# Routed experts of a decoder layer: norm folded into the resident expert weights, turned rows moved by VectorE, a third expert buffer, replies in 4 KB runs

## The chip, the cores and the metric

The kernel runs on one core of a Trainium2 chip. The metric is the device time of one execution in microseconds (us), lower is better. All tensors are float32.

## The reference, cut to what matters

A two-layer decoder on x of 32 batches x 112 tokens x 256 features (3584 tokens). Each layer has a causal attention, an attention over a context of 375 rows, and a feed-forward with experts. The change touches only the last step, the second half of layer 1's feed-forward: 32 experts of 256 -> 128 -> 256, of which each token uses the 4 with the highest score.

```python
x2 = _layernorm(src, ln2_g, ln2_b)           # (s - mean) * rsqrt(var + 1e-5) * g + b
sel = jax.nn.sigmoid(x2 @ sel_w)             # 256 x 32
scores, idx = jax.lax.top_k(sel, K)          # K = 4
gate = (jax.nn.one_hot(idx, E) * scores[..., None]).sum(-2)
h = jax.nn.relu(jnp.einsum('bsd,edh->bseh', x2, keys))      # keys 32 x 256 x 128
moe_out = jnp.einsum('bseh,ehd,bse->bsd', h, values, gate)  # values 32 x 128 x 256
return src + moe_out
```

The output is x + that return value.

## The kernel before, in words

`routed_experts` (line 2488) runs last, in one block with a program per engine. X holds the decoder's residual, S the inner stream (`src`), both resident as 112 partitions x 32 batches x 256. Engines meet only at semaphores, and each engine and each DMA queue takes its program in order. The stage has three parts.

**Choosing and sending.** Eight chunks c of 4 batches. VectorE measures (`measure`, 2740) and normalises without gain and bias (`scale`, 2749), which also adds S to X; the power -0.5 is on GpSimd (`power`, 2586). TensorE turns the rows (2620), ScalarE evicts them with the gain and bias of the norm (2683), TensorE routes (2627), ScalarE takes the sigmoid (2687), VectorE finds the four experts and each token's slot in that expert's region (`choose`, 2760), with two ranking matmuls of TensorE between (2631). ScalarE copies every row four times (2692), VectorE tags the copies with reply place and score (2793, 2794), and GpSimd sends them with indirect DMAs into the table of slots in HBM (`send`, 2590): 16 a chunk, 128 in all, each of 112 rows x 1032 bytes. Meanwhile SP's queue loads the resident `weights` of all 32 experts: 128 partitions x 32 experts x 512 (two halves of keys, 128 each, and 256 of values). The stage starts with SP's small loads; VectorE waits for them (2733) ahead of everything it does.

**The expert tiles.** 143 tiles (`TILES`) of 128 rows. Which expert a tile has is known only at run time, from `table`. For tile j:
- SP: reads the address from the table (2564) and loads 128 x 1032 bytes into one of R = 8 places of `rows` (2569).
- VectorE: reads the expert's number into a register (2822), copies this expert's 128 x 512 weights to one of two buffers `expert` (2824), and takes the minimum that makes the reply addresses (2826). The copy waits for `answered`: the buffer of tile j is free when down(j - 2) is done.
- TensorE: `turn(j)`, two transposes (2648); `up(j)`, two matmuls (2656); `down(j)`, one matmul (2663). A float32 matmul shows as two records. The order is written out: turn(j + 2), up(j + 1), down(j).
- ScalarE: `tile(j)`, two evictions of the turned rows with the norm's gain and bias (2700) into one of two `tileT`; `hide(j)`, the ReLU (2707); `reply(j)`, the scaled eviction of the answer (2712). The order is tile(j + 2), hide(j + 1), reply(j).
- GpSimd: sends the 128 replies with an indirect DMA to their places in HBM (2608).

```python
for j in range(TILES):                 # TensorE, 2669
    if j + 2 < TILES: turn(j + 2)
    if j + 1 < TILES: up(j + 1)
    down(j)
```

**The combine.** When all replies have landed, SP loads the 4 replies of each token of a batch (2575; 112 x 4 runs of 1 KB, 448 KB), six batches ahead; VectorE adds them in three instructions (2832, 2834, 2835), and ScalarE's queue writes the batch out (2727, 112 KB).

Of the kernel before, what the change touches and what calls it, by code (L numbers as in the profile page):

```python
# [26 lines left out]
ACT = mybir.ActivationFunctionType  # L27
# [2460 lines left out]
def routed_experts(nc, G, layer1, W1):  # L2488
# [6 lines left out]
    with ExitStack() as stack:  # L2495
        sb, psum, sem = G["alloc"](stack, "m1")
        weights, route, ln = sb("weights", [P, E, 512]), sb("route", [P, DC, E]), sb("ln", [P, 2, DC])
        rows = sb("rows", [P, 8 * ROOM, D + 2])
        xn, xT = sb("xn", [P, Q, D]), sb("xT", [P, DC, Q * T])
# [13 lines left out]
        expert = [W1["aq"], W1["akc"]]  # L2513
        tileT = [W1["cq"], W1["ck"]]
# [18 lines left out]
        chain_sem, once = sem("chain"), sem("once")  # L2533
        block = stack.enter_context(nc.Block())
# [20 lines left out]
        def _(sp):  # L2555
# [56 lines left out]
        def _(pe):  # L2612
            pe.wait_ge(small_loaded, 16 * len(smalls))
            pe.wait_ge(restart_set, 4)
            for c in range(NC):
# [9 lines left out]
                for i in range(Q):  # L2625
                    for f in range(DC):
# [7 lines left out]
                                 start=False, stop=True).then_inc(ranked, 1)  # L2634

# [15 lines left out]
            def up(j):  # L2651
# [3 lines left out]
                for f in range(DC):  # L2655
                    ins = nc.tensor.matmul(bank[6 + j % 2][:, 0:P], expert[j % 2][:, f * P:(f + 1) * P], tileT[j % 2][:, f, 0:P],  # L2656
# [3 lines left out]
            def down(j):  # L2660
                pe.wait_ge(hidden_ready, j + 1)
                at_least(pe, reply_ready, j - 1)
                nc.tensor.matmul(bank[j % 2][:, 0:D], hidden[j % 2], expert[j % 2][:, DC * P:512],  # L2663
# [13 lines left out]
        def _(act):  # L2677
# [37 lines left out]
            tile(0)  # L2715
            tile(1)
            hide(0)
            for j in range(TILES):
                if j + 2 < TILES:
                    tile(j + 2)  # L2720
# [10 lines left out]
        def _(dve):  # L2731
            chain = Chain(dve, chain_sem, once=once)
            dve.wait_ge(small_loaded, 16 * len(smalls))
            dve.wait_ge(restart_set, 4)
# [25 lines left out]
            def choose(c):  # L2760
                dve.wait_ge(score_ready, c + 1)
# [37 lines left out]
            for c in range(NC):  # L2799
# [3 lines left out]
                if c + 1 < NC:  # L2803
                    scale(c + 1)
# [65 lines left out]
```

## Time and profile before

| | us |
|---|---|
| median of 3 timed runs | 3645.9 (3644.9 to 3647.05) |
| time of the profiled execution | 3625.27 |
| its span, first to last instruction | 3623.5 |
| sending, first to last send (2595) starting | 3106.8 to 3279.5 of the span |
| expert tiles, first to last reply (2712) starting | 3290.3 to 3550.5 |
| combine, first to last addition (2832) starting | 3559.1 to 3617.95 |

Times in a trace are microseconds from the span's start. PE is TensorE's matmul row, PEld its weight loads, DVE VectorE, ACT ScalarE, POOL GpSimd, SP SyncE; a name with q (DVEq, SPq) is the sequencer of that engine, which issues instructions and DMAs. A row of a timeline gives start, duration, engine, line, operation and tiles; what stands in brackets is how long the engine was idle before and what released it.

### The profile page before, as it was taken

What the parts mean: (1) busy time and instruction counts of PE and PEld (TensorE: products, weight loads), DVE (VectorE), ACT (ScalarE), POOL (GpSimd) and SP (SyncE); (2) the same over time, 40 slices, a digit from 0 to 9 for tenths busy, and PEclk for the clock granted to TensorE, in tenths of its full rate; (3) what the DMA queues carried; (4) which work ended last, traced back from release to release, by engine and by line L of the source; (5) the groups of instructions that cost most, each with busy time, mean ns of one, the idle gap of its engine ahead of it and who ended that gap; (6) DMA issues with size and microseconds to landing.
All of it is one profiled execution on the core that took longest, in us unless ns stands there. A gap on an engine that the chain in (4) does not pass through costs nothing. (4 is left out here: it accounts for less than half of the span.)

```text
span 3623.5 us, 79765 instructions
## 1 busy us (share of the span) xinstructions
PE 3014.6 (83%) x28616; PEld 2127.2 (59%) x28616; DVE 2215.9 (61%) x4462; ACT 1774.6 (49%) x3526; POOL 514.2 (14%) x728
## 2 busy tenths in 40 slices
PE   6997999999999978999995799888878998225771
PEld 5885555555555546667774566656647887224551
DVE  4996566666666645667774566656636887552225
ACT  3775555555555532324442344434436887225771
POOL 0000111111111100000000000000001110575551
PEclk9998999999999988999998999999988999558996
DMA  7000544444444410000001333323206776524448
GB/s 174 0 0 22 168 137 137 137 137 137 137 137 137 137 42 1 0 0 1 0 0 38 63 66 67 64 63 67 61 17 202 233 232 187 155 84 128 144 145 226
DMA packets 327192, 351.23 MB, mean 97 GB/s; under 512 B 104552, under 2 KB 304368, under 8 KB 326864
## 3 DMA queue, kind: packets, MB, share of 16 engines
q1 hardware_dynamic: 188304, 174.78, 18.5%
q10 hardware_dynamic: 125680, 140.22, 13.0%
q0 software_dynamic: 13008, 33.56, 2.8%
q8 instruction: 126, 2.06, 0.2%
q14 instruction: 74, 0.61, 0.1%
HBM read 109.49 MB, written 207.08 MB: 87 GB/s over the span
## 5 line engine op out<-in xcount | busy, mean ns | idle before, releaser
L1817 DVE TENSOR_REDUCE x_top<-x_scores 112x4 f32<-112x1500 f32 x128 | 219.9, 1718 | 242.5 <-PE x_scores L1673 239.2
L1054 ACT ACTIVATE x_probs<-x_held,x_minus_top 112x488 f32<-112x488 f32 x256 | 177.5, 694 | 264.4 <-DVE x_minus_top L1111 264.4
L732 POOL TENSOR_TENSOR x_rstd<-x_var,g_minus_half 112x1 f32<-112x1 f32 x128 | 77.9, 609 | 1475.9 <-DVE x_var L728 1008.1
L960 PE MATMUL x_ring<-w_xkv,x_kv 128*122 128x512 f32 x512 | 233.4, 599 | 15.7 <-ACT x_k L844 15.0
L953 PE MATMUL x_ring<-x_kv,w_xkv 128*128 128x488 f32 x512 | 241.6, 596 | 0.0
L1778 ACT ACTIVATE x_probsT<-x_scores 125x1792 f32<-125x1792 f32 x96 | 159.7, 1664 | 147.2 <-PE x_scores L1692 144.6
L844 ACT ACTIVATE x_v<-x_ring 122x512 f32<-122x512 f32 (+1 forms) x224 | 109.8, 506 | 231.7 <-PE x_ring L960 181.4
L1105 DVE SCALAR_TENSOR_TENSOR x_held<-x_scores,x_keep 112x976 f32<-112x976 f32 x128 | 150.4, 1175 | 112.6 <-PE x_scores L973 105.6
L960 PEld LDWEIGHTS x_ring<-w_xkv,x_kv 128*122 128x122 f32 x512 | 92.2, 185 | 137.2 <-issue 94.1
L953 PEld LDWEIGHTS x_ring<-x_kv,w_xkv 128*128 128x128 f32 x512 | 88.0, 191 | 126.2 <-issue 126.0
L2608 POOL DMA_INDIRECT expert_replies<-m_rows,m_reply_of x143 | 137.3, 960 | 135.6 <-DVE m_reply_of L2826 128.4
L1110 DVE TENSOR_REDUCE x_top<-x_held 112x2 f32<-112x976 f32 x128 | 149.7, 1170 | 4.4
L981 PEld LDWEIGHTS x_ring<-g_constants,x_probs 112*122 112x122 f32 x1024 | 109.6, 139 | 71.0 <-issue 65.3
L1673 PE MATMUL x_scores<-x_slots 32*112 32x375 f32 x1024 | 118.3, 531 | 37.1 <-ACT x_probsT L1778 22.4
L2482 DVE SCALAR_TENSOR_TENSOR g_residual<-m_out,m_gate,g_residual 112x256 f32 (+1 forms) x256 | 107.7, 477 | 66.1 <-PE m_out L2326 64.4
L1692 PE MATMUL x_scores<-x_q,x_slots 32*125 32x112 f32 x3072 | 114.1, 286 | 35.4 <-DVE x_top L1817 32.8
L973 PE MATMUL x_scores<-x_k,x_q 64*112 64x488 f32 x512 | 137.8, 615 | 0.8 <-PEq L229 0.8
L2595 POOL DMA_INDIRECT expert_slots<-m_rows,m_slot_of x128 | 129.1, 1009 | 49.2 <-issue 35.9
L1692 PEld LDWEIGHTS x_scores<-x_q,x_slots 32*125 32x125 f32 x3072 | 99.0, 190 | 57.4 <-issue 50.4
L1138 DVE TENSOR_TENSOR x_normed<-x_ring,x_inverse_rows 128x224 f32<-128x224 f32 x64 | 25.1, 391 | 173.4 <-PE x_ring L998 173.4
L981 PE MATMUL x_ring<-g_constants,x_probs 112*122 112x112 f32 x1024 | 120.8, 261 | 5.8 <-ACT x_probsT L844 3.8
L844 ACT ACTIVATE x_probsT<-x_ring 122x448 f32<-122x448 f32 x256 | 123.5, 535 | 0.9 <-PE x_ring L981 0.9
(351 smaller groups left out, 7320.1 us busy)
## 6 DMA issues: line engine op xcount, KB each, us to landing
expert_slots<-d_empty ACTq DMA_DIRECT2D x32, 3612.0 KB, 14.1
by_position<-r_by_position SPq DMA_DIRECT2D x64, 784.0 KB, 4.3
r_bias<-by_position SPq DMA_DIRECT2D x64, 392.0 KB, 3.4
x_ctx<-in_ctx SPq DMA_DIRECT2D x64, 375.0 KB
m_rows<-expert_slots SPq DMA_DIRECT2D x143, 129.0 KB, 2.1
x_kq_swapped<-x_kq_raw ACTq DMA_DIRECT2D x64, 243.5 KB, 3.6
x_slots<-x_kq SPq DMA_DIRECT2D x512, 30.4 KB
m_rows<-expert_replies SPq DMA_DIRECT2D x32, 448.0 KB, 9.7
```

The source lines that it names most:

```text
L844: self.ring.freed(self.nc.scalar.activation(dst, src_of(bank), ACT.Copy), c)
L953: ins = nc.tensor.matmul(bank[:, 0:XK], W["xkv"][:, f, m * P:(m + 1) * P], self.kv[:, f, :], start=(f == 0), stop=(f == DC - 1))
L960: ins = nc.tensor.matmul(bank[0:XCK, :], self.kv[:, f, i * XCK:(i + 1) * XCK], W["xkv"][:, f, 512:1024], start=(f == 0), stop=(f == DC - 1))
L973: ins = nc.tensor.matmul(self.scores[0:T, at:at + XK], self.q[par][half, m, :], self.k[par][half, m, :], start=True, stop=True)
L981: ins = nc.tensor.transpose(bank[0:XCK, i * T:(i + 1) * T], self.probs[u % 4][0:T, i * XCK:(i + 1) * XCK], self.const("ident", T)[:, 0:T])
L1054: nc.scalar.activation(self.probs[u % 4][0:T, :], self.held[m % 2][0:T, i, :], ACT.Exp, scale=self.scale, bias=self.minus_top[0:T, m % 2, ...
L1105: nc.vector.scalar_tensor_tensor(self.held[m % 2][0:T, :, :], self.scores[0:T, 1024 * (m % 2):1024 * (m % 2 + 1)].rearrange("t (i c) -> t ...
L1110: chain.link(nc.vector.tensor_reduce(self.top[0:T, m % 2, :], self.held[m % 2][0:T, :, :], AX_X, ALU.max))
L1692: ins = nc.tensor.matmul(self.scores[0:CK, 512 * a + g * T:512 * a + (g + 1) * T], slots[slot, g, i * CK:(i + 1) * CK], self.q[slot, g, :] ...
L1778: self.nc.scalar.activation(self.probsT[0:CK, i, :, :], self.scores[0:CK, :].rearrange("t (a c) -> t a c", c=512)[:, :, 0:HG * T], ACT.Exp ...
L1817: nc.vector.tensor_reduce(self.top[0:T, g, :], self.scores[0:T, :].rearrange("t (a c) -> t a c", c=512)[:, :, 0:S2], AX_X, ALU.max).then_i ...
L2608: pool.indirect_dma_start(replies[:, :], bass.IndirectOffsetOnAxis(reply_of[:, j:j + 1], 0), rows[:, R + j % R, 0:D], None).then_inc(repli ...
```

## The change

- The norm's gain and bias leave the tiles: `tile` on ScalarE goes, the gain is multiplied into the resident keys (two VectorE instructions in each of chunks 2 to 5), and the bias's part of each hidden unit is made once per expert by 64 matmuls of one column (16 in each of chunks 2 to 5, after the ranking matmuls). Each tile copies its expert's bias column (VectorE), and `hide` adds it in the ReLU. The routing's eviction (2683) keeps gain and bias.
- VectorE moves the turned rows from PSUM to `tileT`, as the last step of a function `bring(j)` that holds all that it does for a tile.
- `expert` has three buffers: the copy for tile j waits for down(j - 3).
- VectorE's wait for the small loads stands in `choose(0)`, after measure and scale of chunk 0.
- The combine's loads land in contiguous 4 KB per token, in place of four runs of 1 KB placed 1032 bytes apart.

```diff
+        groups = rows[:].rearrange("p (g k) d -> p g (k d)", k=K)[0:T, :, 0:K * D]
...
-        expert = [W1["aq"], W1["akc"]]
-        tileT = [W1["cq"], W1["ck"]]
+        expert = [W1["aq"], W1["akc"], sb("expert2", [P, 512])]
+        tileT = [W1[n][:].rearrange("p c n -> p (c n)")[:, 0:D] for n in ("cq", "ck")]
+        bias_of, bias = sb("bias_of", [P, E]), sb("bias", [P, 4])
...
         # SP, combine
-                sp.dma_start(rows[0:T, 4 * g:4 * g + 4, 0:D],
-                             replies[b * T * K:(b + 1) * T * K, :].rearrange("(t k) d -> t k d", k=K)).then_inc(gathered[g], 16)
+                sp.dma_start(groups[:, g, :],
+                             replies[b * T * K:(b + 1) * T * K, :].rearrange("(t k) d -> t (k d)", k=K)).then_inc(gathered[g], 16)
...
         # TensorE, chunk c, after the ranking matmuls
+                if 2 <= c < 6:
+                    if c == 2:
+                        pe.wait_ge(weights_loaded, 16 * len(larges))
+                    for e in range(EG * (c - 2), EG * (c - 1)):
+                        for f in range(DC):
+                            ins = nc.tensor.matmul(bank[7][:, e:e + 1], weights[:, e, f * P:(f + 1) * P], ln[:, 1, f:f + 1],
+                                                   start=(f == 0), stop=(f == DC - 1))
+                    ins.then_inc(folded, 1)
...
         # ScalarE
-            def tile(j):
-                act.wait_ge(tile_turned, j + 1)
-                at_least(act, hidden_full, j - 1)
-                for f in range(DC):
-                    ins = nc.scalar.activation(tileT[j % 2][:, f, 0:P], bank[4 + j % 2][:, f * P:(f + 1) * P], ACT.Identity,
-                                               bias=ln[:, 1, f:f + 1], scale=ln[:, 0, f:f + 1])
-                ins.then_inc(tile_ready, 1)
...
-                nc.scalar.activation(hidden[j % 2], bank[6 + j % 2][:, 0:P], ACT.Relu).then_inc(hidden_ready, 1)
+                nc.scalar.activation(hidden[j % 2], bank[6 + j % 2][:, 0:P], ACT.Relu,
+                                     bias=bias[:, j % 4:j % 4 + 1]).then_inc(hidden_ready, 1)
...
         # VectorE: start, chunk c, tiles
-            dve.wait_ge(small_loaded, 16 * len(smalls))
-            dve.wait_ge(restart_set, 4)
...
+                if 2 <= c < 6:
+                    dve.wait_ge(folded, c - 1)
+                    these = slice(EG * (c - 2), EG * (c - 1))
+                    for f in range(DC):
+                        ins = nc.vector.tensor_scalar(weights[:, these, f * P:(f + 1) * P], weights[:, these, f * P:(f + 1) * P],
+                                                      ln[:, 0, f:f + 1], None, ALU.mult)
+                    ins.then_inc(scaled, 1)
+                    nc.vector.tensor_copy(bias_of[:, these], bank[7][:, these]).then_inc(biased, 1)
...
+            def bring(j):
+                which = dve.value_load(table[0:1, 0, j:j + 1], min_val=0, max_val=E - 1)
+                at_least(dve, answered, j - 2)
+                nc.vector.tensor_copy(expert[j % 3][:], weights[:, bass.ds(which, 1), :].rearrange("p e n -> p (e n)"))
+                nc.vector.tensor_copy(bias[:, j % 4:j % 4 + 1], bias_of[:, bass.ds(which, 1)]).then_inc(expert_ready, 1)
+                dve.wait_ge(loaded[j % R], 16 * (j // R + 1))
+                nc.vector.tensor_tensor(reply_of[:, j:j + 1], rows[:, j % R, D:D + 1], part("limit")[:, j:j + 1],
+                                        ALU.min).then_inc(reply_listed, 1)
+                dve.wait_ge(tile_turned, j + 1)
+                at_least(dve, hidden_full, j - 1)
+                nc.vector.tensor_copy(tileT[j % 2], bank[4 + j % 2][:, 0:D]).then_inc(tile_ready, 1)
```

## Rows read from the trace of the kernel before

**Rows 1.** Windows: PE, PEld, DVE, ACT, POOL busy; clock; DMA share; GB/s.
```profile
3082.00:3281.00 199.00, 50.74 (x232) 43.47 (x232) 92.09 (x346) 45.81 (x57) 137.92 (x140) 0.50 0.39 118
3300.00:3550.00 250.00, 181.45 (x1086) 139.40 (x1086) 72.60 (x272) 196.30 (x543) 130.49 (x137) 1.00 0.47 142
3560.00:3620.00 60.00, 0.00 (x0) 0.00 (x0) 48.54 (x95) 0.00 (x0) 0.00 (x0) 0.50 1.06 288
```
**Rows 2.** Timeline, one tile in the middle of the expert tiles.
```profile
3395.72 0.44 DVE L2824 COPY w_akc<-m_weights 128x512 f32 x1 [1.30 <-PE m_bank L2663]
...
3396.77 0.60 PE L2663 MATMUL m_bank<-w_aq,w_cv 128*128 128x256 f32 x2
3396.84 0.96 POOL L2608 DMA_INDIRECT expert_replies<-m_rows,m_reply_of  x1 [0.91 <-DVE m_reply_of L2826]
...
3397.21 0.38 PE L2648 MATMUL m_bank<-g_constants,m_rows 128*128 128x128 f32 x2
...
3397.52 0.51 DVE L2824 COPY w_aq<-m_weights 128x512 f32 x1 [1.30 <-PE m_bank L2663]
...
3398.13 0.68 PE L2656 MATMUL m_bank<-w_cq,w_aq 128*128 128x128 f32 x4 [0.54 <-issue]
...
3398.65 0.60 PE L2663 MATMUL m_bank<-w_akc,w_cv 128*128 128x256 f32 x2
```
**Rows 3.** All instructions of line 2712 (duration min/median/max, first and last start).
```profile
L2712 ACT ACTIVATE m_rows<-m_bank,m_rows x143: 473/474/477, 3290.3 to 3550.5; 128x256 f32<-128x256 f32 x143
```
**Rows 4.** Timeline, the last two replies: GpSimd with work waiting.
```profile
3551.11 0.96 POOL L2608 DMA_INDIRECT expert_replies<-m_rows,m_reply_of  x1 [0.83 <-ACT m_rows L2712]
3552.37 0.96 POOL L2608 DMA_INDIRECT expert_replies<-m_rows,m_reply_of  x1 [0.30 <-issue]
```
**Rows 5.** Lines 2826 and 2822 (VectorE's minimum, its sequencer) and 2569 (SP's).
```profile
L2826 DVE TENSOR_TENSOR m_reply_of<-m_rows,w_wp x143: 139/141/160, 3285.3 to 3548.5; 128x1 int32<-128x1 f32 x143
L2822 DVEq TENSOR_LOAD <-m_table x143: 299/304/551, 3259.3 to 3546.4; - x143
L2822 DVEq FUSED_REGOPS  x143: 190/190/207, 3259.9 to 3546.7; - x143
L2569 SPq DMA_DIRECT2D m_rows<-expert_slots x143: 332/333/363, 3283.2 to 3537.7; - x143
```
**Rows 6.** Lines 1138 and 1150: VectorE instructions that read PSUM.
```profile
L1138 DVE TENSOR_TENSOR x_normed<-x_ring,x_inverse_rows x64: 383/392/393, 401.6 to 1340.9; 128x224 f32<-128x224 f32 x64
L1150 DVE TENSOR_SCALAR w_ob<-x_ring,x_mv,x_rstd x32: 543/544/547, 425.3 to 1348.2; 112x256 f32<-112x256 f32 x32
```
**Rows 7.** Timeline, sending: GpSimd beside VectorE, chunk 1.
```profile
3129.64 1.22 DVE L2757 TENSOR_TENSOR g_residual<-g_residual,l_stream 112x1024 f32<-112x1024 f32 x1
3129.78 1.76 PE L2620 MATMUL m_bank<-g_constants,m_xn 112*128 112x112 f32 x8 [11.04 <-DVE m_xn L2754]
3129.91 1.77 POOL L2595 DMA_INDIRECT expert_slots<-m_rows,m_slot_of  x1 [0.30 <-issue]
```
**Rows 8.** Line 2036: VectorE, a column of factors, one input in SBUF.
```profile
L2036 DVE TENSOR_SCALAR r_xn<-l_stream,r_rstd x32: 343/344/354, 2720.2 to 3039.3; 112x256 f32 x24, 112x256 f32<-112x256 f32 x8
```
**Rows 9.** Timeline, TensorE's weight loads at the half clock.
```profile
3290.94 0.93 PEld L2656 LDWEIGHTS m_bank<-w_cq,w_aq 128*128 128x128 f32 x4 [0.62 <-issue]
```
**Rows 10.** Timeline, the start of the stage.
```profile
3082.27 0.20 POOL L2580 MEMSET w_ao<- 128x128 f32 x1 [46.68 <-POOLq L260]
...
3086.71 1.40 DVE L2742 BATCH_NORM_STATS2 m_stats<-l_stream 112x6 f32<-112x256 f32 x4 [5.35 <-DMA m_ln<-in_L_ffn_ln_b]
...
3106.82 1.16 POOL L2595 DMA_INDIRECT expert_slots<-m_rows,m_slot_of  x1 [11.14 <-DVE m_rows L2794]
```
**Rows 11.** Timeline, the combine: first addition, one without a wait, last.
```profile
3559.12 0.69 DVE L2832 TENSOR_TENSOR m_rows<-m_rows 112x512 f32<-112x512 f32 x1 [10.43 <-DMA m_rows<-expert_replies]
...
3617.95 0.69 DVE L2832 TENSOR_TENSOR m_rows<-m_rows 112x512 f32<-112x512 f32 x1
```
**Rows 12.** Who waited for whom, from 3556 us to the end.
```profile
DVE m_rows L2832 <- DMA m_rows<-expert_replies: 18.8, 27, 10.4
```

More of the change, by code:

```diff
@@ L2533, in routed_experts @@
         chain_sem, once = sem("chain"), sem("once")
+        folded, biased, scaled = sem("folded"), sem("biased"), sem("scaled")
+        EG = E // 4
         block = stack.enter_context(nc.Block())
@@ L2655, in up @@
                 for f in range(DC):
-                    ins = nc.tensor.matmul(bank[6 + j % 2][:, 0:P], expert[j % 2][:, f * P:(f + 1) * P], tileT[j % 2][:, f, 0:P],
+                    ins = nc.tensor.matmul(bank[6 + j % 2][:, 0:P], expert[j % 3][:, f * P:(f + 1) * P], tileT[j % 2][:, f * P:(f + 1) * P],
                                            start=(f == 0), stop=(f == DC - 1))
@@ L2662, in down @@
                 at_least(pe, reply_ready, j - 1)
-                nc.tensor.matmul(bank[j % 2][:, 0:D], hidden[j % 2], expert[j % 2][:, DC * P:512],
+                nc.tensor.matmul(bank[j % 2][:, 0:D], hidden[j % 2], expert[j % 3][:, DC * P:512],
                                  start=True, stop=True).then_inc(answered, 1)
@@ L2713, in reply @@
                                      scale=rows[:, j % R, D + 1:D + 2]).then_inc(reply_ready, 1)
-            tile(0)
-            tile(1)
             hide(0)
             for j in range(TILES):
-                if j + 2 < TILES:
-                    tile(j + 2)
                 if j + 1 < TILES:
@@ L2760, in choose @@
             def choose(c):
+                if c == 0:
+                    dve.wait_ge(small_loaded, 16 * len(smalls))
+                    dve.wait_ge(restart_set, 4)
                 dve.wait_ge(score_ready, c + 1)
@@ L2820, in _ @@
             dve.wait_ge(weights_loaded, 16 * len(larges))
-            for j in range(TILES):
-                which = dve.value_load(table[0:1, 0, j:j + 1], min_val=0, max_val=E - 1)
-                at_least(dve, answered, j - 1)
-                nc.vector.tensor_copy(expert[j % 2][:], weights[:, bass.ds(which, 1), :].rearrange("p e n -> p (e n)")).then_inc(expert_ready, 1)
-                dve.wait_ge(loaded[j % R], 16 * (j // R + 1))
-                nc.vector.tensor_tensor(reply_of[:, j:j + 1], rows[:, j % R, D:D + 1], part("limit")[:, j:j + 1], ALU.min).then_inc(reply_listed, 1)
+            dve.wait_ge(scaled, 4)
+            dve.wait_ge(biased, 4)
+            def bring(j):
[9 more added lines that the diff above has]
+                nc.vector.tensor_copy(tileT[j % 2], bank[4 + j % 2][:, 0:D]).then_inc(tile_ready, 1)
+            for j in range(TILES):
+                bring(j)
             dve.wait_ge(summed, NC)
@@ L2831, in _ @@
                 dve.wait_ge(gathered[g], 16 * (b // 6 + 1))
-                chain.link(nc.vector.tensor_tensor(rows[0:T, 4 * g:4 * g + 2, 0:D], rows[0:T, 4 * g:4 * g + 2, 0:D],
-                                                   rows[0:T, 4 * g + 2:4 * g + 4, 0:D], ALU.add))
-                chain.link(nc.vector.tensor_tensor(X[0:T, b, :], X[0:T, b, :], rows[0:T, 4 * g, 0:D], ALU.add))
-                nc.vector.tensor_tensor(X[0:T, b, :], X[0:T, b, :], rows[0:T, 4 * g + 1, 0:D], ALU.add).then_inc(added, 1)
+                chain.link(nc.vector.tensor_tensor(groups[:, g, 0:2 * D], groups[:, g, 0:2 * D], groups[:, g, 2 * D:4 * D], ALU.add))
+                chain.link(nc.vector.tensor_tensor(X[0:T, b, :], X[0:T, b, :], groups[:, g, 0:D], ALU.add))
+                nc.vector.tensor_tensor(X[0:T, b, :], X[0:T, b, :], groups[:, g, D:2 * D], ALU.add).then_inc(added, 1)
 _TRANSPOSED = {"v_wT": "L0_attn_v_w", "o_wT": "L0_attn_o_w", "x_qT": "L1_xattn_Wq", "x_kT": "L1_xattn_Wk",
```

## The prediction

> **What bounds the kernel now.** I cut the stage into its three parts first [rows 1]. The window of the expert tiles shows no engine full: in 250 us ScalarE is busy 196.3, PE 181.5, GpSimd 130.5, VectorE 72.6. With nothing full, a ring of waits must set the pace, so I read the timeline of one tile [rows 2]. down(j) starts at 3396.77 and lasts 0.60; VectorE's expert copy, idle for 1.30, is released by it at 3397.52; it ends at 3398.03; up(j+2) starts 0.10 later; the next down, behind this up, starts at 3398.65. So each tile pays down 0.60 + hop 0.15 + copy 0.51 + hop 0.10 + up, start to the down behind it, 0.52 = 1.88 us, with the shorter copies of the other tiles (0.44) some 1.80. The rows of the scaled eviction give the mean: (3550.5 - 3290.3) / 142 = 1.832 us a tile [rows 3]. Two buffers make that ring: copy(j+2) needs down(j), and down(j+1) stands on PE behind up(j+2).
>
> In the sending part GpSimd is busy 137.9 of 199 us [rows 1], and the gap behind each send is 0.30 [rows 7]: with 128 gaps and the start of the stage taken off, it has no time to spare. The combine is paced by VectorE and its loads: 31 steps take 3617.95 - 3559.12 = 58.8 us, 1.898 each [rows 11], of which 18.8 - 10.4 = 8.4 us are waits for loads after the first [rows 12].
>
> **The tiles after the change.** The old ring opens: copy(j+3) needs down(j), and behind up(j+3) on PE stands down(j+2). It now gives two tiles: down 0.60 + 0.15 + what `bring` does + 0.06 to 0.10 + 0.52. In `bring` between the wait and the tile's release are the expert copy 0.44 to 0.51 [rows 2], the bias copy and the minimum, 0.14 each [rows 5], and the copy of 256 columns out of PSUM. That last one no row has. From below, an addition that reads 224 columns there takes 0.392; from above, a two-factor scaling of 256 takes 0.544 [rows 6]; I take 0.42, near the simpler instruction. Sum 1.14 to 1.33, so the ring is 2.43 to 2.70 us for two tiles: 1.22 to 1.35 a tile, less what the copies overlap.
>
> Four other limits stand close to it.
> - GpSimd: the last two replies show it with work waiting: 3552.37 - 3551.11 = 1.26 us a reply [rows 4]. 143 replies cannot go faster; this is the floor.
> - PE: up 0.52 and down 0.44, start to start [rows 2]; for the two transposes, whose successor always waited, 0.25 (two starts 0.11 apart within a 0.38 row) to 0.38. 1.21 to 1.34 at the full clock that it has in this window [rows 1].
> - VectorE: 1.14 to 1.33 of work, and its sequencer's register load 0.30 + 0.19 [rows 5] can run beside the last copy.
> - SP: 0.33 to issue a load [rows 5] and a register load that I take like VectorE's, 0.30 + 0.19, together 0.82 and small steps: about 1.0.
>
> ScalarE loses two evictions, 2 x 0.45, and keeps under 0.8; a bias operand in the ReLU I cost at nothing, as these 2 x 0.45 rows carried one. DMA works at share 0.47 now [rows 1]; at 1.3 us a tile that is 0.47 x 1.832 / 1.3 = 0.66, and loads are eight tiles ahead, so I cost it at nothing; if that cover went, PE's transposes would be late next. I take GpSimd's 1.26 and 0.05 for meetings with VectorE: **1.31 us a tile**, bounds 1.26 and 1.50. Gain 142 x (1.832 - 1.31) = **74.1 us** (81.2 to 47.1). Also the first tile's two evictions, 0.81, become minimum and copy: 0.4 us gained.
>
> Where the bound 1.50 comes from: in these rows the expert copy that started 0.68 us into a reply's send took 0.51, and others took 0.44 [rows 2], so the two meet somewhere, and a send that began inside VectorE's 1.22 us addition took 1.77 where replies take 0.96 and ended only 0.82 us after that addition [rows 7]. Serial sums are 0.96 + 0.51 = 1.47 a tile. But the copy started while the send ran and lost only 0.07, so the send holds what they share for about the first 0.75 us; 0.75 + 0.44 = 1.19 still fits under 1.26. The Trainium skill (SBUF — State Buffer, the sections on the shared port) speaks against this change: a Vector copy in a two-port mode and a GpSimd instruction exclude each other for the whole instruction, and descriptor writing stops. By it the sum would have the serial 1.47; in the trace the copy starts before the send has ended, so I keep it as a rival.
>
> **The folding.** PE gets 16 matmuls a chunk, of two records each: 32 weight loads of 0.93 / 4 = 0.23 us at the half clock [rows 9], 7.5 us. PE idles 11.0 us ahead of the next chunk's transposes [rows 7], which follow exactly there, so I cost them at nothing; beyond 11.0 the transposes would be late. VectorE gets two scalings of 1024 columns and a small copy. A one-factor scaling of 256 takes 0.344 [rows 8]. If it were one column a cycle like the 1.22 us addition of 1024, a scaling is 1.2; if it runs at twice that, as the row hints (an addition of 224 takes 0.392), 0.75. Both lie ahead of the next `choose`, in an idle stretch of some 3 us. What costs is that GpSimd cannot begin a send inside them: the addition above cost it some 1.77 - 0.96 = 0.81. Four chunks with one such meeting of 0.75: **3.0 us lost**, between 0 and two meetings each of 0.7, 5.6.
>
> **The start.** VectorE begins at 3086.71, held 5.35 us by the small loads, while the block starts about 3082.3 [rows 10]. The measuring, the power and the scaling now run in these 4.4 us; PE and ScalarE still wait for the loads, at the same 3086.7, and by then the rows are ready but for 0.5. First send at 3102.4 in place of 3106.82, and GpSimd paces the rest: **4.4 us gained**, 4.0 to 4.6. The queues are moved past nothing.
>
> **The combine.** VectorE's three instructions are unchanged in size: 0.69 + 0.43 + 0.42 and gaps, 58.8 less 8.4 = 50.4 for 31, 1.63 each. If loads were never late the gain is 8.4; if run length did nothing, 0. The loads queue six deep at 288 GB/s [rows 1], so bytes are what they wait for, and longer runs drop three of four packets. I take 1.70 a step: **6.1 us gained**. The Trainium skill (DMA: Bandwidth & Descriptors, Specifications) puts line rate at runs of 512 B and more; by it 1 KB is long enough and the gain would be 0. No row here has these loads in other runs.
>
> **Sum**: 74.1 + 0.4 + 4.4 + 6.1 - 3.0 = 82.0. The profiled execution took 3625.3 and would take 3543.3; the timed median stands 20.6 above it (0.57%), and nothing says that this belongs to what goes, so 3645.9 - 82.0 = **3563.9 us**.
>
> **Rivals.**
> - A, the forecast: GpSimd's queue sets the tiles, 1.31. Chance 0.59.
> - B, as A, but the combine gains nothing, bytes and not packets being its limit: 3645.9 - 75.9 = 3570.0. For it: 448 + 112 KB in 1.9 us is already 300 GB/s. Against: it is not VectorE's floor. 0.18.
> - C, VectorE and GpSimd exclude each other, 1.50 a tile and 5.6 lost in the folding: 47.1 + 0.4 + 4.4 + 6.1 - 5.6 = 52.4, 3593.5. For it: the 1.77. Against: the copy within a send. 0.17.
> - D, the change does not do what it says: the ring is closed again by the second `tileT` buffer at 1.83, as both copies now stand in one queue. Gain 7.9: 3638.0. Against: up(j+1), which frees it, is two tiles back. 0.02.
> - E, slower: VectorE becomes the bound with nothing overlapping. A register load of 0.52, copies 0.51 + 0.14 + 0.14 + 0.54 and two hops of 0.15 are 2.15 us; with 0.12 of address steps 2.27. That is 142 x 0.44 = 62 us more, less 7.9: 3700. It decides from 1.832 + 7.9 / 142 = 1.89 us a tile. Against: the register load has ended long before VectorE is released, after 1.30 us idle [rows 2]. 0.04.
>
> A measurement of this kernel tells 0.2%, 7.3 us, from no change. Faster by more: A to D, 0.95 with the edge of D taken off; within: 0.01; slower: E, 0.04. The range 3548 to 3592 takes in A's bounds (1.26 a tile, combine 8.4, nothing lost: 3551.4, and 3 us for the unknown gap between profile and median), B, and all of C but its end.
>
> **What would show it.** Right: replies (2712) 1.26 to 1.36 apart, GpSimd's gaps near 0.30 there with the releaser no longer VectorE's minimum, VectorE's wait ahead of the expert copy gone or short, the PSUM copy near 0.42; first send near 3102; combine steps near 1.70. Wrong: sends (2608) longer than 0.96 or expert copies longer than 0.51 on average (C); replies over 1.4 apart with VectorE busy or its sequencer loading (E); TensorE's transposes in chunks 3 to 6 late after the folding.

## The result, and the profile after

Timed side by side, the changed kernel took 3627.3 us (median of 5, 3625.0 to 3631.7) and the kernel before 3644.9 (median of 5, 3640.7 to 3647.1). The ratio is 0.9962, with a 95% interval of 0.9946 to 0.9978: 17.6 us gained by the medians, 14 by the ratio, where I forecast 82.0, and outside my range. The profiled execution took 3627.28 us, span 3625.5. That of before took 3625.27, 20 us less than its timed runs, so between the two profiles nothing is gained: the after one is 2.0 us longer.

The windows of the three parts (sending, tiles, combine), columns as in [rows 1]:
```profile
3078.00:3302.00 224.00, 77.57 (x360) 70.69 (x360) 97.68 (x359) 45.29 (x57) 135.68 (x139) 0.50 0.35 104
3313.00:3557.00 244.00, 189.96 (x1130) 150.45 (x1128) 129.16 (x560) 113.17 (x285) 136.44 (x141) 0.95 0.50 151
3566.00:3620.00 54.00, 0.00 (x0) 0.00 (x0) 46.98 (x94) 0.00 (x0) 0.00 (x0) 0.50 1.02 317
```
Sending got longer, the tiles only a little shorter, and still no engine is full in the tiles: VectorE went from 72.6 us busy in 250 to 129.2 in 244, ScalarE from 196.3 to 113.2. GpSimd, which I wanted full, is busy 136 of 244 us.

Lines of the kernel after (duration min/median/max in ns, first and last start): scaled eviction, replies, PSUM copy, scaling of the keys, ReLU with bias.
```profile
L2717 ACT ACTIVATE m_rows<-m_bank,m_rows x143: 465/474/477, 3313.5 to 3556.9; 128x256 f32<-128x256 f32 x143
L2612 POOL DMA_INDIRECT expert_replies<-m_rows,m_reply_of x143: 954/960/1162, 3314.8 to 3559.2; - x143
L2844 DVE COPY w_cq<-m_bank x72: 410/417/426, 3308.6 to 3554.6; 128x256 f32<-128x256 f32 x72
L2811 DVE TENSOR_SCALAR m_weights<-m_weights,m_ln x8: 746/750/754, 3165.3 to 3247.6; 128x1024 f32<-128x1024 f32 x8
L2711 ACT ACTIVATE w_cv<-m_bank,m_bias x143: 358/367/370, 3311.4 to 3555.8; 128x128 f32<-128x128 f32 x143
```
The prices of single instructions are as costed: the copy out of PSUM 0.417 (I took 0.42), the scaling 0.75, a reply 0.960 in the median. The ReLU, which I cost at no more than before, takes 0.367 for 0.277. The pace is not as costed: (3556.9 - 3313.5) / 142 = 1.714 us a tile, where I forecast 1.31 and [rows 3] gave 1.832.

Start and combine, answering to [rows 10, 11]:
```profile
3077.84 0.20 POOL L2584 MEMSET w_ao<- 128x128 f32 x1 [47.46 <-POOLq L260]
...
3098.11 1.16 POOL L2599 DMA_INDIRECT expert_slots<-m_rows,m_slot_of  x1 [11.24 <-DVE m_rows L2796]
...
3565.46 0.69 DVE L2853 TENSOR_TENSOR m_rows<-m_rows 112x512 f32<-112x512 f32 x1 [10.48 <-DMA m_rows<-expert_replies]
...
3619.98 0.68 DVE L2853 TENSOR_TENSOR m_rows<-m_rows 112x512 f32<-112x512 f32 x1
```
From the first memset to the first send it is 20.27 us in place of 24.55, 4.3 gained. The combine takes 54.5 / 31 = 1.758 a step in place of 1.898, 4.3 gained.

The loss is in the sending: 128 sends in 203.9 us (3098.1 to 3302.0) where before needed 172.6. The timeline from 3137 us, with the folding's last matmuls, the transposes, GpSimd's last send of this chunk, and what starts after it ("remote" in brackets: a semaphore event ended the wait, but no instruction ended near it):
```profile
3137.80 0.99 PE L2644 MATMUL m_bank<-m_ln,m_weights 128*128 128x1 f32 x4
...
3143.20 1.75 PE L2624 MATMUL m_bank<-g_constants,m_xn 112*128 112x112 f32 x8 [4.41 <-DVE m_xn L2753]
...
3161.60 0.94 POOL L2599 DMA_INDIRECT expert_slots<-m_rows,m_slot_of  x1 [0.30 <-issue]
3165.28 1.42 DVE L2811 TENSOR_SCALAR m_weights<-m_weights,m_ln 128x1024 f32<-128x1024 f32 x2 [21.00 <-remote]
3166.08 1.34 ACT L2695 ACTIVATE m_xT<-m_bank,m_ln 128x448 f32<-128x448 f32 x2 [31.88 <-remote]
...
3180.09 1.07 POOL L2599 DMA_INDIRECT expert_slots<-m_rows,m_slot_of  x1 [10.16 <-DVE m_rows L2796]
```
TensorE's last matmul of this chunk's folding ended at 3138.79. VectorE, which waits for that alone and has been idle for 21.0 us, starts 26.5 us later. ScalarE starts late too, after transposes that ended near 3144.9. In between GpSimd has sent without a break, 0.30 us from one send to the next; both are released 2.7 and 3.5 us after its last send ended, and GpSimd, out of work, has by then begun 17.5 us of idling. The same comes again at 3245 us (17.4 us). In the tiles it shows in small: 40 of the 143 ReLUs start over 0.3 us after the matmul that releases them has ended, in the profile before none. I call these **late releases**: TensorE's matmul has ended, and the engine waiting for it is released late. The trace also records the increments of the semaphores, and they put the delay into the increment, not into the waiting engine: that of the folding's semaphore stands at 3165.26, 26.5 us after the last matmul of the folding and 0.02 ahead of VectorE's start. The granted clock is 0.50 in the sending both before and after; in the tiles it is 0.95 for 1.00.

The 2.0 us between the spans add up: layers before 4.4 shorter, start 4.3, tiles 142 x (1.832 - 1.714) = 16.8, the step from them to the combine 0.1 and the combine 4.3 gained; sending 31.3 and the step from it to the tiles 0.6 lost.

### The profile page after: what moved, and what is told of

The parts are those of the page before. It is cut to its first block and busy times, and to the rows that moved or that the text cites. A ratio compares the mean times of both kernels' runs of the same rounds, so it can differ in the third digit from the quotient of the medians.

```text
span 3625.5 us, 80177 instructions
## 1 busy us (share of the span) xinstructions
PE 3037.6 (84%) x28744; PEld 2155.7 (59%) x28744; DVE 2276.2 (63%) x4760; ACT 1681.0 (46%) x3240; POOL 514.7 (14%) x728
## 5 line engine op out<-in xcount | busy, mean ns | idle before, releaser
L1054 ACT ACTIVATE x_probs<-x_held,x_minus_top 112x488 f32<-112x488 f32 x256 | 177.5, 694 | 264.3 <-DVE x_minus_top L1111 264.3
```

Of the source, the lines that this page charges most:

```text
L1054: nc.scalar.activation(self.probs[u % 4][0:T, :], self.held[m % 2][0:T, i, :], ACT.Exp, scale=self.scale, bias=self.minus_top[0:T, m % 2, ...
```

## The experiments

They went to several chips, each set with its own timed runs of the kernel before beside it. Two conditions came up, on the same kernels: in some sets no late releases, in others (also the first timing) many. One of the chips showed both, in different sets, so it is not the chip alone. I say "prompt" and "late" for them below. The table gives medians in us; in set x and for z's fourth kernel it is one timed run, elsewhere 2 to 11. The sets were run in the order of the table.

| set | condition | before | kernels |
|---|---|---|---|
| first timing | late | 3644.9 | changed 3627.3 |
| x | prompt | 3633.8 | x1 3549.4, x2 3625.9, x3 3551.0, x4 3527.7 |
| y | prompt | 3621.3 | changed 3536.1, y6 3533.8 |
| z | prompt | 3622.7 | changed 3542.7, z2 3534.6, z3 3546.6, before 3624.4 |
| w | prompt | 3621.1 | changed 3542.6, w2 3539.9 |
| v | late | 3636.3 | changed 3631.8, v2 3608.3 |
| u | late | 3646.4 | before 3639.9, u2 3555.4 |
| t | late | 3646.4 | t1 3621.7, t2 3607.6 |

**Set x: what in the change is slow?** x1 takes the 64 folding matmuls out of the changed kernel and sets the hidden bias to zero (the norm's bias is left out); the scalings stay.
```diff
...
-                    for e in range(EG * (c - 2), EG * (c - 1)):
-                        for f in range(DC):
-                            ins = nc.tensor.matmul(bank[7][:, e:e + 1], ...)
-                    ins.then_inc(folded, 1)
...
-                    nc.vector.tensor_copy(bias_of[:, these], bank[7][:, these]).then_inc(biased, 1)
+                    nc.vector.memset(bias_of[:, these], 0.0).then_inc(biased, 1)
```


> The changed kernel without the 64 one-column matmuls of the folding; the scalings stay, the bias of the hidden units is left out (set to zero). Theory H (TensorE's semaphore increments are held back while GpSimd issues sends one behind the other, once TensorE has done a long run of matmuls beside them): the two stalls of 20 us and the one of 6 us in the sending part go, first to last send takes 170 to 176 us in place of 203.9, and the tiles keep their pace of about 1.70 us, since nothing changes there. Rival W (VectorE's scalings of the weights keep the port from GpSimd or delay VectorE itself): the sending part stays above 190 us.

Measured: 84 us faster than before, sending 177.4, but tiles at 1.261: the slow tiles were gone with matmuls that had ended long before them, which no theory of mine had. x2 puts the same 64 matmuls alone into the kernel before.

> The kernel before with the 64 one-column matmuls of the folding added on TensorE and nothing else (their result is not used). Theory H: the sending part, 172.7 us before, grows by 20 to 35 us, with stalls in which TensorE has finished and VectorE and ScalarE still wait; the tiles stay at 1.83 us. Rival W: no change, within 2 us of 172.7, because the matmuls fit into the 11 us that TensorE idles.

Measured: sending 172.4 us, tiles 1.830, no late release, so theory H fell here. The matmuls cost what I had costed, in TensorE's idle time:
```profile
3138.37 6.82 PE L2641 MATMUL m_bank<-m_ln,m_weights 128*128 128x1 f32 x32
```
x3 is the kernel before with the third buffer alone.
```diff
-        expert = [W1["aq"], W1["akc"]]
+        expert = [W1["aq"], W1["akc"], sb("expert2", [P, 512])]
...
-                at_least(dve, answered, j - 1)
+                at_least(dve, answered, j - 2)
```


> The kernel before with three expert buffers and nothing else. If the ring of two buffers is what paced the tiles, the next limit is ScalarE with 0.80 + 0.28 + 0.47 us of evictions and its gaps: 1.58 to 1.65 us a tile in place of 1.83, some 30 us gained, with few late releases, as GpSimd then still has gaps of over 0.6 us between its replies. If late releases of TensorE's increments depend on TensorE's own density, they show here too and the pace stays above 1.70.

Measured: 82.8 us gained, 1.242 a tile; far more than I expected by then. x4 is the changed kernel with each tile's replies written in one piece by a plain DMA of ScalarE's queue, GpSimd idle in the tiles. It leaves out the placing of the replies: the same bytes are moved, but the combine adds wrong rows. (The edit also makes SP wait for VectorE's last minimum ahead of the combine.)
```diff
-                pool.indirect_dma_start(replies[:, :], bass.IndirectOffsetOnAxis(reply_of[:, j:j + 1], 0),
-                                        rows[:, R + j % R, 0:D], None).then_inc(replied[j % R], 16)
+                act.dma_start(replies[j * P:(j + 1) * P, :], rows[:, R + j % R, 0:D]).then_inc(replied[j % R], 16)
...
```


> The changed kernel with the replies of the tiles written by plain DMAs of ScalarE's queue, one behind the other, in place of GpSimd's indirect ones: the same bytes, in the wrong places, and GpSimd idle in the tiles. Theory H: no late releases are left, replies come 1.2 to 1.3 us apart in place of 1.70, 60 us gained. Rival: if VectorE's copies out of PSUM or the ring over three buffers set the pace, it stays above 1.5 us a tile.

Measured: 1.216 a tile, 106 us gained. But its sending part, with the folding unaltered and nothing else changed there, took 177.5 us, and had none of the stalls. Four kernels had shown no late release at all, one of them in a part where it equals the changed kernel. So the changed kernel itself had to be run again.

**Set y: the changed kernel again.** y6 is x3 with the 4 KB runs and the early measure: the change without folding and with ScalarE still moving the turned rows.

> The changed kernel again, unaltered, on the chip of this call. In the first four runs neither half of the change showed the two stalls of 20 us among the sends nor the slow tiles that the whole change shows: the stalls are absent wherever GpSimd or the folding's matmuls are taken out, and absent also in the sending part of the kernel with direct replies, which has the folding unaltered. If the stalls and the slow tiles belong to the kernel (late releases by TensorE beside back-to-back sends), this run shows them again: 3620 to 3635 us, sending 200 us or more, tiles 1.65 or more. If they belong to one execution or one chip, it shows sending 177.5 us, tiles 1.26 to 1.31 and 3545 to 3560 us.

> The kernel before with the third expert buffer, the replies in 4 KB runs and the early measure, without the folding and with ScalarE moving the turned rows: the change without its half on ScalarE and VectorE. Theory: no late releases, since TensorE has no folding and its transposes wait on ScalarE as before; tiles 1.24 us, sending 172.5 us, a combine step 1.75 to 1.90, the start 4.3 us earlier: 3540 to 3546 us where the third buffer alone took 3551. Rival, that what slows the changed kernel comes with the earlier start (the sends then meet the chunks' other work at another phase): sending over 180 us and tiles over 1.4.

The changed kernel took 3536.1 us, ratio 0.9767 (0.9751 to 0.9784): 85 us gained. Its lines and the combine's first and last addition:
```profile
L2717 ACT ACTIVATE m_rows<-m_bank,m_rows x143: 474/475/480, 3286.3 to 3464.9; 128x256 f32<-128x256 f32 x143
L2612 POOL DMA_INDIRECT expert_replies<-m_rows,m_reply_of x143: 956/962/1215, 3287.5 to 3472.5; - x143
L2599 POOL DMA_INDIRECT expert_slots<-m_rows,m_slot_of x128: 937/942/3090, 3098.0 to 3275.5; - x128
```
```profile
3478.58 0.69 DVE L2853 TENSOR_TENSOR m_rows<-m_rows 112x512 f32<-112x512 f32 x1 [16.19 <-DMA m_rows<-expert_replies]
...
3527.27 0.69 DVE L2853 TENSOR_TENSOR m_rows<-m_rows 112x512 f32<-112x512 f32 x1
```
The scaled evictions come (3464.9 - 3286.3) / 142 = 1.258 us apart. GpSimd, which is the limit here, is slower: (3472.5 - 3287.5) / 142 = 1.303 us a reply, with its usual gap of 0.31 and a mean of 0.996 for the reply itself. ScalarE runs ahead of it as far as the eight places for answers let it: GpSimd begins the first reply 1.2 us after the first eviction and the last one 7.6 us after the last. So the combine starts 13.7 us after the last eviction, where it was 8.6 before: what the 1.258 gains beyond GpSimd's 1.303 is paid back there. "A tile" below stays the distance of the evictions. Sending 177.5; combine 1.571. The two traces start the stage within 0.15 us of each other and send first at 3098.1 and 3098.0, so neither the phase nor the work explains the 91 us. Here the increment of the folding's semaphore stands at 3138.70, 0.02 us after the last matmul of that folding; the granted clock of the sending is 0.50 here too. Set x had run in this same condition, and what it seemed to say of the folding (x1) was the condition's doing. y6 took 3533.8, ratio 0.9762 (0.9746 to 0.9779): tiles 1.249 (GpSimd's replies 1.281), sending 172.5, combine 1.521. It came out under the 3540 that I expected at least, by its combine.

**Set z: the parts beside each other.** z2 is y6 again, z3 is x3.

> The changed kernel once more, beside three others on one chip. It took 3627 us where it was first timed and 3536 us in the run before this one, with the same instructions. Theory: the 91 us belong to the chip or the place, not to the kernel's own order of work, and come as late releases by TensorE; so this run takes either about 3536 (sending 177.5 us, tiles 1.26) or about 3627 (sending 204, tiles 1.71), alike in all its executions on this chip. Rival, that it falls differently from execution to execution: values between, or both in one set of executions.

> The kernel before with third buffer, 4 KB runs and early measure, beside the changed kernel. If the chip shows no late releases: within 5 us of the changed kernel, 3530 to 3540. If it does: theory that they need TensorE's matmuls beside back-to-back sends only, then its tiles are slow too (over 1.5 us a tile), 3580 or more; rival that they need what the folding adds, then it stays at tiles of 1.25 and beats the changed kernel by 60 to 90 us.

> The third expert buffer alone, on the same chip as the three others. Against the kernel with 4 KB runs and early measure it shows what these two bring: 4.4 us at the start, and in the combine between 0 (run length does nothing) and 31 x (1.90 - 1.52) = 12 us; so 4 to 17 us slower than that kernel. Rival, that the fast combine of that run belonged to the chip: only 4 us slower.

> The kernel before, for its profile on the same chip as the three others: sending 172.6 us, tiles 1.832 us, and a combine step of 1.90 to 2.0 us. If its combine step here is under 1.7, the fast combine belongs to the chip and not to the 4 KB runs.

Prompt again. Of the 80.0 us that the changed kernel gained, the third buffer alone brings 76.2 (ratio 0.9788, 0.9770 to 0.9805); 4 KB runs and early measure 12.0 more (start 4.3; combine 2.078 to 1.788 a step, 9.0); the folding with VectorE's move costs 8.1 (2.3 in set y), 4.9 of them in the sending. z4, the kernel before, has sending 172.5, tiles 1.833 and a combine step of 1.851, so the faster combine does not belong to the chip. The combine is noisy between sets: over all profiles a step of 1 KB runs takes 1.800 to 2.078 (6 profiles, mean 1.935) and one of 4 KB runs 1.521 to 1.904 (14, mean 1.681). That is 31 x 0.254 = 7.9 us, and in each of the three later sets that profiled both (x, z, u) every 4 KB step is the shorter one.

**Set w: what lengthens the sending.** w2 leaves out matmuls, scalings and the hidden bias (so the norm's gain and bias are missing in the tiles).
```diff
-                        ins = nc.vector.tensor_scalar(weights[:, these, f * P:(f + 1) * P], ...,
-                                                      ln[:, 0, f:f + 1], None, ALU.mult)
...
+            chain.link(nc.vector.memset(bias_of[:], 0.0))
```


> The changed kernel unaltered, to find the condition in which it took 3627 us: on two other chips it took 3536 and 3543. On a chip like those: sending 177.5 us, tiles 1.26. Where it shows sending over 195 and tiles over 1.6 instead, the kernel beside it (no folding at all) tells whether the folding's matmuls are needed for that.

> The changed kernel without the folding's matmuls and without the scalings: hidden bias zero and the norm's gain and bias left out of the experts' input. Theory: the changed kernel's sending part is 5 us longer than that of the kernel before (177.5 against 172.5) because eight sends begin inside a scaling of 1.4 us on VectorE, as I costed it; without them sending is 172.5 and the sum of the sends 129.0 in place of 133.9, the tiles stay at 1.26, and the kernel is 5 us faster than the whole change on this chip. Rival: it is the folding's matmuls that hold the chunks back, or the early measure: sending stays 177.5, as it did without the matmuls.

Sending went from 177.4 to 172.6 us, as expected; the time fell by 2.7 us, less than the 5 expected, with two timed runs of each. The lines show why the sending did: first the longest send of w2 (1.767), then the changed kernel beside it, VectorE's addition, a send and the two scalings.
```profile
L2599 POOL DMA_INDIRECT expert_slots<-m_rows,m_slot_of x128: 937/942/1767, 3099.5 to 3272.1; - x128
```
```profile
3151.22 1.22 DVE L2756 TENSOR_TENSOR g_residual<-g_residual,l_stream 112x1024 f32<-112x1024 f32 x1
...
3151.51 3.07 POOL L2599 DMA_INDIRECT expert_slots<-m_rows,m_slot_of  x1 [0.30 <-issue]
3152.36 1.41 DVE L2811 TENSOR_SCALAR m_weights<-m_weights,m_ln 128x1024 f32<-128x1024 f32 x2
```
The send begins inside the addition and ends 0.81 us after the second scaling, while VectorE runs on with a small copy and the next measuring; one such send in each of four chunks, not the eight that I expected, 4 x (3.07 - 1.76) = 5.2. The Trainium skill (SBUF — State Buffer, the part on two separate sides) says that a VectorE instruction with two SBUF inputs or in a two-port mode and a GpSimd one exclude each other, and that whichever starts first has the port pair for its whole instruction. The trace agrees for the addition, which started first; that the send also stood behind both scalings, which started after it, is more than that sentence says. In the tiles it is a small term: beside four VectorE instructions a tile the median reply keeps 0.96, but 35 of y5's 143 take over 1.0, up to 1.215 (1 of 143 in the kernel before), and the mean is 0.996 for 0.960.

**Set v: the late condition comes up.** v2 is y6 once more.

> The changed kernel unaltered, again to find the condition of its first timing. If that condition comes up: 3620 to 3635 us, sending over 195, tiles over 1.6. If not: 3535 to 3545, sending 177.5, tiles 1.26, the fourth set of executions to show that.

> The kernel with the third buffer, the 4 KB runs and the early measure and without the folding, beside the changed kernel. If the condition comes up: theory that it needs the folding's matmuls or VectorE's part in the tiles, sending 172.5 and tiles 1.25 here all the same; rival that it strikes any kernel whose tiles run at 1.3 us, tiles over 1.5 here too. If it does not come up: 3528 to 3540 us, level with the changed kernel or up to 10 us ahead of it.

The changed kernel: 3631.8, ratio 0.9987 (0.9970 to 1.0004), sending 199.0, tiles 1.731. v2: 3608.3, ratio 0.9923 (0.9880 to 0.9966), sending 181.1, tiles 1.714, though it has neither folding nor VectorE's move. So the rival holds: it strikes both kernels with fast tiles. In the sending it strikes the one with the folding harder, by 17.9 us in this set. One tile of v2:
```profile
3297.51 0.60 PE L2664 MATMUL m_bank<-w_akc,w_cv 128*128 128x256 f32 x2
...
3298.61 0.96 POOL L2609 DMA_INDIRECT expert_replies<-m_rows,m_reply_of  x1 [0.30 <-issue]
...
3300.31 0.48 ACT L2713 ACTIVATE m_rows<-m_bank,m_rows 128x256 f32<-128x256 f32 x1 [0.45 <-remote]
3300.42 0.43 DVE L2826 COPY w_akc<-m_weights 128x512 f32 x1 [2.44 <-remote]
...
3301.54 0.96 POOL L2609 DMA_INDIRECT expert_replies<-m_rows,m_reply_of  x1 [1.97 <-DVE m_reply_of L2828]
```
The down matmul ends at 3298.11. VectorE, idle for 2.44 us, starts 2.3 us after it; ScalarE starts 2.2 us after it, of which it was idle for the last 0.45 (its eviction of turned rows had itself started 0.5 us after the transposes). Both starts stand 0.7 to 0.9 us after the fourth of GpSimd's close sends has ended. GpSimd then misses work for 1.97 us. Over the stage 25 of its 142 gaps are over 1.3 us, 2.06 on average, where y6 has none between its replies. The mean gap is 0.74 for y6's 0.31, and that is the whole difference of GpSimd's paces, 1.716 for 1.281. A lower clock does not explain it: the granted clock is 0.98 in these tiles.

**Set u: who needs to be there.** u1 is the kernel before, u2 is x4.

> The kernel before, profiled. Where it takes 3636 to 3645 us, theory: its sends show one or two stalls of 5 to 20 us in which GpSimd has ended its sends and ScalarE or VectorE starts late after a matmul that has ended, while its tiles keep 1.83 us, since GpSimd pauses 0.9 us after every reply. Rival: no stall at all, and its time lies elsewhere (combine, the layers before). Where it takes about 3621, sending 172.6 and tiles 1.832 as before.

> The changed kernel with the replies written by plain DMAs of ScalarE's queue (each tile's rows in one piece, so the replies stand in the wrong places and the combine adds wrong rows), GpSimd idle in the tiles. On a chip where the changed kernel is slow, theory that the late releases need GpSimd's sends: sending 195 to 204 us with its stalls, but tiles at 1.2 to 1.3 us. Rival, that they come from TensorE's own dense work or from the loads, whoever sends the replies: tiles at 1.5 or more. On the other chips 1.22 a tile, as in its first run.

Late. The kernel before has two stalls in the sending too (GpSimd idle for 8.7 and 7.4 us; 184.5 in place of 172.6), and tiles at 1.850. Chunk 3's routing matmuls and what they release, first in u1:
```profile
3150.69 3.20 PE L2627 MATMUL m_bank<-m_route,m_xT 128*112 128x32 f32 x16 [0.82 <-ACT m_xT L2683]
...
3166.51 0.94 POOL L2595 DMA_INDIRECT expert_slots<-m_rows,m_slot_of  x1 [0.30 <-issue]
3166.74 0.28 ACT L2687 ACTIVATE w_rq<-m_bank 112x128 f32<-112x128 f32 x1 [16.10 <-DMA g_residual<-in_x]
...
3176.12 1.07 POOL L2595 DMA_INDIRECT expert_slots<-m_rows,m_slot_of  x1 [7.59 <-DVE m_rows L2794]
```
and the same two in z4, the same kernel in the prompt condition:
```profile
3154.64 3.19 PE L2627 MATMUL m_bank<-m_route,m_xT 128*112 128x32 f32 x16 [0.81 <-ACT m_xT L2683]
...
3157.88 0.28 ACT L2687 ACTIVATE w_rq<-m_bank 112x128 f32<-112x128 f32 x1 [3.28 <-PE m_bank L2627]
```
From matmul end to sigmoid it is 12.85 us in u1 and 0.05 in z4, and u1's increment is recorded at 3166.71, just ahead of the sigmoid. (The releaser that u1's row names, a load of the first layer, is the view's guess.) Its release comes 0.23 us into the last send of the chunk. u2 in the same set, replies and sends:
```profile
L2713 ACT ACTIVATE m_rows<-m_bank,m_rows x143: 466/474/479, 3314.8 to 3487.9; 128x256 f32<-128x256 f32 x143
L2600 POOL DMA_INDIRECT expert_slots<-m_rows,m_slot_of x128: 937/942/1761, 3101.2 to 3303.4; - x128
```
Its sending has the stalls (202.2 us), its tiles do not: (3487.9 - 3314.8) / 142 = 1.219, as in the prompt condition (1.216). TensorE's work is the same in both parts as in the changed kernel; what is missing in the tiles are GpSimd's sends. In the tiles, then, the late releases need them; one profile and two timed runs say so, and what in a send it is (the writing of its descriptors, its indirect addresses) they do not separate.

**Set t: does the number of sends in a row count?** t1 is y6, t2 is y6 with
```diff
+                if j % 4 == 3:
+                    pool.memset(pause[:], 0.0).then_inc(paused, 1)
+                    pool.wait_ge(paused, j // 4 + 1)
```


> Third buffer, 4 KB runs and early measure, for comparison with the kernel beside it. Where the kernel before takes 3636 us or more: tiles about 1.71 us, sending 181, 3600 to 3620 us. Where it takes 3621: tiles 1.25, sending 172.5, 3530 to 3540.

> The same kernel, with a GpSimd memset of 128 x 384 (0.4 to 0.5 us) and its wait after every fourth reply, so that no more than four replies follow each other at 0.30 us gaps. Without the condition GpSimd bounds the tiles and each group of four costs 4 x 1.26 + 0.6 = 5.64, 1.41 a tile, 20 us slower than its neighbour. With the condition, theory that late releases need five or more sends in a row and fall out at a pause: tiles 1.41 to 1.5 us, 30 to 40 us faster than its neighbour. Rival, that a memset is no pause, or that the count does not matter: tiles 1.7 or more, no faster than its neighbour.

Late. t1 took 1.781 a tile, t2
```profile
L2717 ACT ACTIVATE m_rows<-m_bank,m_rows x143: 467/483/529, 3292.7 to 3539.1; 128x256 f32<-128x256 f32 x143
```
1.735. A memset just ahead of a send does not prevent it:
```profile
3333.91 0.43 POOL L2613 MEMSET m_pause<- 128x384 f32 x1
...
3334.62 0.96 POOL L2610 DMA_INDIRECT expert_replies<-m_rows,m_reply_of  x1 [0.28 <-issue]
...
3336.13 0.43 DVE L2830 COPY w_akc<-m_weights 128x512 f32 x1 [2.64 <-remote]
...
3337.25 1.17 POOL L2610 DMA_INDIRECT expert_replies<-m_rows,m_reply_of  x1 [1.67 <-DVE m_reply_of L2832]
```
Gaps of GpSimd over 1.3 us fell from 29 to 18, but the tiles stayed above 1.7, so my theory of four sends in a row fell. (In this set the new kernels have 3 and 2 timed runs.) By time t2 stands 14 us ahead, but the ratios' intervals overlap (0.9877 to 0.9978 and 0.9861 to 0.9933), so I claim no gain.

## Why the prediction was wrong

**What failed.** The step is the pace of the tiles, "I take GpSimd's 1.26 and 0.05 for meetings with VectorE: 1.31 us a tile". It held the sum's largest term, 74.1 us; in the first timing the pace was 1.714 and the term 16.8. It took for granted that an engine learns of a finished matmul in 0.04 to 0.15 us whatever GpSimd does. I had read those hops from tiles in which GpSimd pauses 0.83 to 0.91 us after every reply [rows 2, 4], and the change takes just that pause away. The second step is the folding, "3.0 us lost", bounds 0 and 5.6: the sending got 31.3 longer. Here the cover that I named, TensorE's idle 11.0 us, held (6.82 us of matmuls, nothing behind them late by them), but VectorE's next measuring now stands behind a release by TensorE. When that is 26.5 us late, the whole chain of the next chunk still lies ahead of the next send: 14.8 us from release to send, against 9.4 in the kernel before, whose late release comes further down the chain (3166.74 to 3176.12). So the folding did not make the late releases, but doubled their price: stalls of 17.5 and 17.4 us against 8.7 and 7.4. The late traces agree: sending 199.0 to 203.9 in the three with the folding, 178.9 to 185.6 in the four without.

**The sign that I had.** The profile before stood 20.6 us under its timed runs. I wrote that nothing says that this belongs to what goes. u1 shows two stalls that lengthen the sending by 11.9 us, and before took 3636 to 3646 us in the three later sets whose profiles show late releases, 3621 to 3634 in the four whose profiles don't. (Single runs overlap: set v goes down to 3628, set z up to 3629, and set x has one run, of 3634.) That the first timing of before ran in the late condition and its profile in the prompt one fits, but is inferred: no profile exists of those runs.

**What held**, where the releases are prompt:
- GpSimd as the limit: its replies come 1.303 to 1.304 us apart in the three prompt profiles of the changed kernel, against 1.31, and in place of 1.836 before: 142 x 0.533 = 75.8 us where I had 74.1. The 0.05 for meetings with VectorE is there too, as 0.036 in the mean reply. The evictions, by which I had wanted to judge, come 1.258 to 1.259 apart, under my floor of 1.26, because ScalarE runs ahead; their 81.5 us are not all gained.
- The third buffer is what opens the ring. VectorE's move brings nothing: GpSimd's replies come 1.281 to 1.289 us apart with ScalarE moving the rows (4 profiles) and 1.293 to 1.304 with VectorE (5), so it costs some 2 us. I had not priced the third buffer by itself, and it would have carried the sum.
- Folding 4.9 lost in the sending, in the bounds 0 to 5.6, by the mechanism named; the meetings were longer than I had them, 1.31 each and not 0.75.
- Start 4.3 for 4.4. Combine 7.9 over all kernels for 6.1, 4.3 in the first timing. The rule by which it would gain nothing (the Trainium skill, DMA: Bandwidth & Descriptors, Specifications) was my rival B: the runs speak against it, with means of 1.935 and 1.681 a step.
- Sum: 85, 80 and 79 us in three prompt sets, for 82.0; in the late ones the same kernel gained 18 and 5. So the forecast fits one condition, and knew of no other. That the sum comes so close is in part luck: tiles (1.7 us more), combine (1.8 more) and folding (1.9 more lost) err in part against each other, and the combine varies from set to set by more than that.

**Rivals.** C fell: the median reply kept 0.960 to 0.962 (mean 0.97 to 1.00), and even the late tiles have the expert copy at 0.43. D fell: the ring did open. E fell: VectorE is busy 129 of 244 us. The 1.714 was none of them.

**What stays open.** What the late condition is, and why TensorE's releases show it and no others that the traces let one check: in the tiles of the late profile after, TensorE's own matmuls start at most 0.06 us after the copy or ReLU that they waited for. GpSimd's replies start 0.76 us (median) after the eviction that they waited for, as they do in the kernel before. Events of semaphores are partly missing in those traces (in the tiles of the profile after, 114 of 143 are recorded for the up matmuls and 107 for the down ones), so single increments can't be followed everywhere. That the length of the row of sends counts is neither shown nor excluded. A kernel without GpSimd's indirect sends that still places its replies rightly was not tried.

**The better version.** y6 (third buffer, 4 KB runs, early measure, norm kept in ScalarE's evictions) beats or ties the changed kernel in every set that has both: 3533.8 to 3536.1, 3534.6 to 3542.7, and under late releases 3608.3 to 3631.8. It beats the kernel before by 2.4% or more in the prompt sets and by 0.8% in set v.

## What to carry to other kernels

Split a change before pricing it as a whole: where releases were prompt, one extra buffer gave 76 of the 80 us, and the rework around it cost work in another part and made a wait longer. Where one engine runs ahead of the one that is the limit, read the pace from the limit's own rows. A profile that stands 20 us off the timed median of its own kernel is a finding to be explained, not a remark. And where a change packs GpSimd's sends closer together, the hops from TensorE to its readers have to be counted as a risk, best with few waits on TensorE ahead of work that feeds the sends.

## What the hardware showed that I had not expected

- A finished matmul's release can reach ScalarE and VectorE 2 us late and more in the tiles and 12.85 to 26.5 us late in the sending, with GpSimd's indirect DMAs following each other at 0.30 us. The same code gave 0.05 in other sets. With the sends gone from the tiles it did not come there (1.219 us a tile), while the sending of the same execution stalled.
- The same program takes 3536 to 3543 or 3627 to 3632 us by this for the greater part, its timed runs within a set agreeing to 0.4%. Of the 92.7 us between the spans of the profile after and y5, the combine is 5.8.
- An indirect send that begins inside VectorE's addition of 1024 columns takes 1.76 us. Where two scalings of 1024 columns follow the addition without a break it takes 3.07 and ends 0.81 us after the second, though VectorE is busy on with other work.
